# Two-layer graph kernel: the next batch's input rows are turned by VectorE in 32x32 blocks, after a blocked load, instead of by TensorE

## What is computed

```
feats  = einsum(x, W0)                       # 8 heads x 64 units
e      = leaky_relu(self_i + neigh_j, 0.2);  att = softmax(e where adj)
x1     = layernorm(x + relu(att @ feats + b))
agg    = (adj @ x1) / max(deg, eps)
out    = layernorm(x1 + relu([x1, agg] @ W1.T))
```

## Time and profile before

| | us |
|---|---|
| three runs | 3256.30, 3260.62, 3260.65; median 3260.62 |
| the profiled execution's own time | 3259.45 |
| its span, first to last instruction | 3257.7 |
| PE busy, of the span | 3198.1 |
| DVE busy | 2351.7 |
| ACT busy | 2095.9 |
| mean granted TensorE clock | 0.997 |

### The profile page before, as it was taken

One profiled execution on the slowest core, in us unless ns is written; L12 is line 12 of the kernel. 1 busy time (PEld: TensorE's weight loads), 2 busy tenths in 40 slices (PEclk: granted clock), 3 DMA queues, 4 the chain that ended last, 5 costly groups with the idle time before them and its releaser, 6 DMA issues.

```text
span 3257.7 us, 124901 instructions
## 1 busy us (share of the span) xinstructions
PE 3198.1 (98%) x56896; PEld 2698.7 (83%) x56896; DVE 2351.7 (72%) x4272; ACT 2095.9 (64%) x2712; POOL 283.6 (9%) x251
## 2 busy tenths in 40 slices
PE   7999999999999999999999999999999999999998
PEld 6969789697896978979788797987969879697895
DVE  6858678586785857859588585876858768586685
ACT  5748567485674947749477494765837658485583
POOL 0010200102011020100202002020020200202001
PEclk8999999999999999999999999999999999999999
DMA  6143151431524225251242513415144251331512
GB/s 217 58 114 102 51 159 66 109 98 51 154 68 118 87 60 157 62 133 65 78 141 63 140 56 94 129 58 146 51 102 120 58 147 62 102 115 51 140 33 49
DMA packets 368657, 314.52 MB, mean 97 GB/s; under 512 B 285056, under 2 KB 285056, under 8 KB 368128
## 3 DMA queue, kind: packets, MB, share of 16 engines
q1 hardware_dynamic: 368128, 306.52, 33.8%
HBM read 205.26 MB, written 34.08 MB: 73 GB/s over the span
## 4 chain that ended last, share of the span: by engine, by line
PE 89%; DVE 6%; issue 2%; ACT 2%; DMA 1%; SPq 0%; DVEq 0%; POOL 0%; ACTq 0%
PE six L940 77%; PE pair L940 11%; DVE mask L769 2%; PE six L964 1%; DVE rest L674 1%; PE pair L964 1%; DVE x_parts L669 1%; ACT step L512 1%; DMA s_bc<-self_scores 1%; ACT trh L477 0%; DVE x_parts L697 0%; DVE trl L708 0%; DMA self_scores<-sc_row 0%; DVE feat L699 0%; DVE trl L905 0%
## 5 line engine op out<-in xcount | busy, mean ns | idle before, releaser
L940 PE MATMUL six<-rows_bf,mask 128*128 128x65 bf16 x45056 | 1507.8, 193 | 19.3 <-DVE mask L769 12.6
L940 PEld LDWEIGHTS six<-rows_bf,mask 128*128 128x128 fp8e4 x45056 | 1497.6, 97 | 27.5 <-DVE mask L769 16.0
L512 ACT ACTIVATE step<-s_bc,n_step 128x1024 uint16<-128x1024 f32 x1024 | 1090.3, 1136 | 90.7 <-DVE mask L769 71.3
L769 DVE TENSOR_TENSOR mask<-adj_t,step 128x1024 uint16<-128x1024 uint16 x1024 | 655.2, 685 | 47.9 <-ACT step L512 47.4
L940 PE MATMUL six<-adj_t,x_parts 128*128 128x512 fp8e4 x1536 | 385.5, 380 | 11.1 <-DVE trl L905 5.4
L455 POOL TENSOR_TENSOR s_bc<-feat,rden 128x512 f32<-128x512 f32 x112 | 124.1, 1113 | 2721.3 <-DVE s_bc L818 2707.1
L940 PEld LDWEIGHTS six<-adj_t,x_parts 128*128 128x128 f16 x1536 | 145.9, 98 | 201.5 <-DVE trl L905 13.2
L477 ACT ACTIVATE mask<-six,rdeg 128x512 f32<-128x512 f32 x128 | 87.9, 686 | 237.5 <-PE six L940 237.5
L940 PE MATMUL six<-w1h,trh 128*128 128x512 f32 x512 | 211.6, 413 | 0.0
L477 ACT ACTIVATE trh<-six 128x512 fp32r<-128x512 f32 x160 | 87.9, 598 | 184.5 <-PE six L940 162.4
L940 PE MATMUL six<-w1h,trl 128*128 128x512 f32 x512 | 201.0, 392 | 0.0
(11 more groups left out here) (127 smaller groups left out, 4922.8 us busy)
## 6 DMA issues: line engine op xcount, KB each, us to landing
s_bc<-self_scores SPq DMA_DIRECT2D x128, 512.0 KB, 3.8
mask<-in_adj_dram SPq DMA_DIRECT2D x64, 512.0 KB, 4.1
adj_nat<-in_adj_dram SPq DMA_DIRECT2D x64, 512.0 KB, 3.5
xs<-in_x_dram SPq DMA_DIRECT2D x128, 256.0 KB, 3.9
out_dram<-mask SPq DMA_DIRECT2D x128, 256.0 KB, 3.3
adj_nat<-in_x_dram SPq DMA_DIRECT2D x64, 256.0 KB, 5.8
step<-in_x_dram SPq DMA_DIRECT2D x64, 256.0 KB, 4.2
xs<-in_L_gnn_W_dram SPq DMA_DIRECT2D x1, 2048.0 KB, 13.2
```

Of the source, the lines that this page charges most:

```text
L512: act.activation(step[:, g % STEP_SLOTS], s_bc[:, h % 2], ACT.Sigmoid, scale=STEP, bias=n_step[:, jt, h:h + 1]).then_inc(stepped.sem, 1)
L769: dve.tensor_tensor(mask[:, g % MASK_SLOTS], adj_t[:, jt, :], step[:, g % STEP_SLOTS], ALU.logical_shift_left).then_inc(masked.sem, 1)
L940: return pe.matmul(o, l, r, start=start, stop=stop, skip_group_check=True)
```

## The change

Each load of an x tile for turning becomes 4 loads, one for each 128 features, into 32 partitions each: partition 32k + r gets, for i = 0 to 3, row 32i + r of features 128k to 128k + 127, in runs of 512 bytes. DVE's `transpose` in place then turns each 32x32 block of the 128x512 tile. The result has features {128k + 32c + j} on partition 32k + j of chunk c, so layer one's weights are loaded in that order: 16 loads instead of 4. `x_high` and `x_low` read the turned tile in SBUF; PE's `turn_x` is gone. Of DVE's and ACT's order: the block turn stands behind mask 13, 21, 29 and 37, `x_high` behind step g + 5, `x_low` behind mask g + 2, where each had stood at other places before. In the tail DVE's turns stand in `ln1(t)` for t = 1, 2, 5, 6. In the prologue DVE turns tiles 0 to 3 ahead of the weights' split, and 4 to 7 behind the first feature rows.

```diff
-    XT_BANKS = (6, 7, 6, 7, 0, 1, 0, 1)
-    TURN_AT = (10, 13, 18, 21)
+    TURN_AT = (13, 21, 29, 37)
+    SPLIT_BEHIND = 2
+    TAIL_TURN_AT = (1, 2, 5, 6)
+    Q = P // KC
...
+        def turned_rows(t):
+            rows_of = lead_x[:, t] if t < HALF else tail_x[:, t - HALF]
+            return rows_of.rearrange("p (i c r) -> p c i r", i=KC, c=KC)
+        def by_blocks(rows_of):
+            return rows_of.rearrange("p c (i r) -> p c i r", i=KC)
...
+            def load_blocks(rows_of, b, t, landed):
+                for k in range(KC):
+                    sp.dma_start(rows_of[k * Q:(k + 1) * Q].rearrange("p (i f) -> p i f", i=KC),
+                                 x[b, t * P:(t + 1) * P, col(k)].rearrange("(i r) f -> r i f", i=KC)
+                                 ).then_inc(landed.sem, 16)
...
             for c in range(KC):
-                sp.dma_start(w_raw[:, c, :].rearrange("p (h u) -> p h u", h=H),
-                             gat_w[:, col(c), :].rearrange("h p u -> p h u")).then_inc(w_in[0], 16)
+                for k in range(KC):
+                    features_at = k * P + c * Q
+                    sp.dma_start(w_raw[k * Q:(k + 1) * Q, c, :].rearrange("p (h u) -> p h u", h=H),
+                                 gat_w[:, features_at:features_at + Q, :].rearrange("h p u -> p h u")
+                                 ).then_inc(w_in[0], 16)
...
             for s in range(2):
-                sp.wait_ge(xt_ps.sem, xt_ps.at(0, 2 * s + 2))
+                sp.wait_ge(xt_lo.sem, xt_lo.at(0, 2 * s + 2))
                 load_adj(0, s)
...
-                    if h in (3, 4):
-                        s = h - 3
-                        sp.wait_ge(xt_ps.sem, xt_ps.at(b + 1, 2 * s + 2))
+                    if h in (4, 6):
+                        s = h // 2 - 2
+                        sp.wait_ge(xt_lo.sem, xt_lo.at(b + 1, 2 * s + 2))
                         load_adj(b + 1, s)
...
             def x_high(b, t):
-                act.wait_ge(xt_ps.sem, xt_ps.at(b, t + 1))
-                copy(trh[:, :, col(t % HALF)],
-                     bank[XT_BANKS[t]][:].rearrange("p (k n) -> p k n", k=KC)).then_inc(xt_hi.sem, 1)
+                act.wait_ge(x_turned_ok.sem, x_turned_ok.at(b, t + 1))
+                copy(by_blocks(trh[:, :, col(t % HALF)]), turned_rows(t)).then_inc(xt_hi.sem, 1)
...
+            def turn_blocks(b, t):
+                source, landed = (lead_x[:, t], lead_in[t]) if t < HALF else (tail_x[:, t - HALF], tail_in[t - HALF])
+                dve.wait_ge(landed.sem, landed.at(b, 16 * KC))
+                dve.transpose(source, source).then_inc(x_turned_ok.sem, 1)
...
                     mask_word(g)
-                    if more and g - 7 in TURN_AT:
-                        x_low(b + 1, TURN_AT.index(g - 7))
+                    if more and g in TURN_AT:
+                        turn_blocks(b + 1, TURN_AT.index(g))
+                    if more and g - SPLIT_BEHIND in TURN_AT:
+                        x_low(b + 1, TURN_AT.index(g - SPLIT_BEHIND))
```

More of the change, by code:

```diff
@@ L69, in gat_sage_kernel @@
     W1_BANKS = (2, 3)
-    XT_BANKS = (6, 7, 6, 7, 0, 1, 0, 1)
     FT_BANKS = (0, 1, 4, 5, 4, 6, 4, 5)
     MAX_BANK = 3
-    TURN_AT = (10, 13, 18, 21)
+    TURN_AT = (13, 21, 29, 37)
+    SPLIT_BEHIND = 2
+    TAIL_TURN_AT = (1, 2, 5, 6)
+    Q = P // KC
+    assert Q == 32
     FIRST, SECOND = slice(0, HALF), slice(HALF, T)
@@ L216, in gat_sage_kernel @@
         x_in = [Signal(sem(f"x_in{t}"), 16) for t in range(T)]
-        lead_in = [Signal(sem(f"lead_in{t}"), 16) for t in range(HALF)]
-        tail_in = [Signal(sem(f"tail_in{t}"), 16) for t in range(HALF)]
+        lead_in = [Signal(sem(f"lead_in{t}"), 16 * KC) for t in range(HALF)]
+        tail_in = [Signal(sem(f"tail_in{t}"), 16 * KC) for t in range(HALF)]
         a_in = [Signal(sem(f"a_in{s}"), 32) for s in range(4)]
@@ L224, in signal @@
             return Signal(sem(name), per_batch)
-        xt_ps = signal("xt_ps", T)
+        x_turned_ok = signal("x_turned_ok", T)
         xt_hi = signal("xt_hi", T)
@@ L309, in _ @@
         def _(sp):
+            def load_blocks(rows_of, b, t, landed):
[3 more added lines that the diff above has]
+                                 ).then_inc(landed.sem, 16)
             def load_lead(b, t):
-                sp.dma_start(lead_x[:, t, :], x[b, t * P:(t + 1) * P, :]).then_inc(lead_in[t].sem, 16)
+                load_blocks(lead_x[:, t, :], b, t, lead_in[t])
             load_lead(0, 0)
             for c in range(KC):
-                sp.dma_start(w_raw[:, c, :].rearrange("p (h u) -> p h u", h=H),
-                             gat_w[:, col(c), :].rearrange("h p u -> p h u")).then_inc(w_in[0], 16)
+                for k in range(KC):
[3 more added lines that the diff above has]
+                                 ).then_inc(w_in[0], 16)
             for t in range(1, HALF):
@@ L328, in load_tail @@
             def load_tail(b, t):
-                sp.dma_start(tail_x[:, t - HALF, :], x[b, t * P:(t + 1) * P, :]).then_inc(tail_in[t - HALF].sem, 16)
+                load_blocks(tail_x[:, t - HALF, :], b, t, tail_in[t - HALF])
             def load_adj(b, t):
@@ L541, in batch @@
                     make_step(g)
-                    if more and g - 9 in TURN_AT:
-                        if g - 9 == TURN_AT[0]:
+                    turned_at = g - STEP_SLOTS - 1
+                    if more and turned_at in TURN_AT:
+                        if turned_at == TURN_AT[0]:
                             act.wait_ge(ft_ps.sem, ft_ps.at(b, T))
-                        x_high(b + 1, TURN_AT.index(g - 9))
+                        x_high(b + 1, TURN_AT.index(turned_at))
                 def x1_parts_of(t):
@@ L632, in _, with weight_parts @@
         def _(dve):
[L634 to L637, removed]
+            def weight_parts():
+                dve.wait_ge(w_in[0], 16 * KC * KC)
+                dve.tensor_copy(w0h[:], w_raw).then_inc(w_ready, 1)
+                dve.wait_ge(w_ready, 1)
+                dve.tensor_tensor(w0l[:], w_raw, w0h[:].bitcast(F32), ALU.subtract).then_inc(w_ready, 1)
             def attention_weights():
@@ L707, in x_low @@
                 c = t % HALF
-                dve.tensor_tensor(trl[:, :, col(c)], bank[XT_BANKS[t]][:].rearrange("p (k n) -> p k n", k=KC),
-                                  trh[:, :, col(c)].bitcast(F32), ALU.subtract).then_inc(xt_lo.sem, 1)
+                dve.tensor_tensor(by_blocks(trl[:, :, col(c)]), turned_rows(t),
+                                  by_blocks(trh[:, :, col(c)]).bitcast(F32), ALU.subtract).then_inc(xt_lo.sem, 1)
             def feature_rows(b, t):
@@ L882, in ln1 @@
                         x_low(b + 1, T - 1)
+                    if more and t in TAIL_TURN_AT:
+                        turn_blocks(b + 1, HALF + TAIL_TURN_AT.index(t))
                     dve.wait_ge(o2_sb.sem, o2_sb.at(b, t + 1))
@@ L922, in _ @@
             for t in range(HALF):
+                turn_blocks(0, t)
+            weight_parts()
+            for t in range(HALF):
                 x_low(0, t)
@@ L928, in _ @@
                 feature_rows(0, t)
+            for t in range(HALF, T):
+                turn_blocks(0, t)
             for t in range(HALF, T):
@@ L956, in split_product @@
                 return ins
[L958 to L965, removed]
             def features(b, t, chunks=range(KC)):
@@ L1039, in batch @@
                     for jt in range(T):
-                        if more and h * T + jt in TURN_AT:
-                            turn_x(b + 1, TURN_AT.index(h * T + jt))
                         if h < 2 and jt == HALF:
@@ L1129, in batch @@
                         own(t + 1)
[L1130 to L1133, removed]
             pe.wait_ge(consts, N_CONST)
-            for t in range(HALF):
-                turn_x(0, t)
             pe.wait_ge(w_ready, 2)
@@ L1143, in _ @@
             pe.wait_ge(ft_sb.sem, ft_sb.at(0, 2))
-            for t in range(HALF, T):
-                turn_x(0, t)
             pe.wait_ge(w_in[3], 16)
```

## The result

The changed kernel takes 3266.73 us against 3259.88 (medians of 20 runs each), a ratio of 1.0021 with a 95% interval of 1.0014 to 1.0028: 0.2% slower. One of the changed kernel's 20 runs had a granted clock of 0.782 and took 3735.49 us; the ratio leaves it out, and without it the median is 3266.41. The forecast was +11 us; it is +6.9, and +10.5 between the two profiled spans (3268.2 and 3257.7).

What follows compares the result with a forecast made beforehand. The prediction took PE as the bound, with DVE setting its pace between key tiles 13 and 29. Key tiles +26, tail -24 and prologue +8 on 3259.45 gave 3269.5, as a median 3271 us; range 3248 to 3306.

Steps and rivals of the forecast that it cites:

- The bound: Key tiles 13 to 29: DVE sets PE's pace there; removing the turns is worth at most 2.4 us a batch.
- Key tiles: Key tile stage: DVE waits 1.22 us for `x_high`, a turned head takes 12.66 us; +1.75 a batch, +26 us.
- second way of reckoning: Key tiles: 93.9 without turns plus 4 x (12.66 - 11.6) gives 98.1 against 96.3 us, +1.8 a batch.
- The block turn: DVE's transpose of 128x512 f32: taken as 0.605 us from the nearest row, bounds 0.27 and 1.24.
- Rival (B): DVE in turned heads: the block turn takes twice as long, 1.24 us; 38 us more, 3309 us; chance 0.14.
- the estimate 0.65: DVE's block turn by the Trainium skill's figure: 0.65 us, which would make the sum 2.7 us higher.
- Tail: Tail of each batch: four PE turns of 0.44 us go; -1.6 us a batch, x 15 = -24 us.
- Rival (A): Key tiles: DVE's 11.43 us a head fits under PE's 11.6, all PE turns are won; 3206 us; chance 0.14.
- SP's queue: Load queue: 24 more loads a batch, the tail's 16 at 0.44 us each, cost nothing.
- rival (C): Tail: the 16 loads, at 0.79 us or more each, hold up x1; 1.4 us a batch, 3292 us; chance 0.08.
- Prologue: Start, once: 36 more loads ahead of adjacency tiles 0 and 1, first words near 29.7; +8 us, 0 to +13.
- The sum: Whole kernel: 3259.45 + 26 - 24 + 8 = 3269.5 for the profiled execution, 3271 us as median.

Runs made afterwards that it cites:

- split4: The changed kernel with `x_low` two masks later, behind mask g + 4 instead of g + 2: 3214.10 us, ratio 0.9856 to the kernel before.
- split5: The changed kernel with `x_low` behind mask g + 5 instead of g + 2: 3208.95 us, ratio 0.9845 to the kernel before.
- tail_only: The kernel before with only tiles 4 to 7 loaded in blocks and turned by DVE, weights in their old order: 3235.16 us, ratio 0.9920.
- loads_only: The kernel before, PE turns kept, with each x tile for turning in 4 loads and layer one's weights in 16: 3270.64 us, ratio 1.0031.
- extra_pass: The changed kernel with one more 128x512 DVE pass behind each block turn among the key tiles: 3303.56 us, ratio 1.0132 to the kernel before.

## Why the prediction held, point by point

- *The bound.* Right: the stage between the turns is where DVE sets PE's pace. In the kernel before, PE's waits for a mask lie where the working put them, most of them ahead of tile 29 (up to 1.1 us of idle time). The last batch's key tiles, 93.9 us, served as the measure of that stage without turns; with the wait gone the 15 batches come within 0.6 us of it, block turns and all. It is a rough measure: the last batch takes 93.2 to 97.7 us over the twelve profiles, with idle times of PE that end with nothing the profile shows.
- *Key tiles.* Forecast +1.75 us a batch from a turned head of 12.66 us; measured +1.50, heads of 12.61. Batch 4 alone is 98.0, as the second way of reckoning had it (98.1). The rise of the mean is smaller, since the kernel before takes 0.45 us more in its mean batch (96.75) than in batch 4, which the working took for all, and the changed kernel only 0.25 more (98.25).
- *The block turn.* Taken as 0.605 from the nearest form; 0.63 to the next instruction. Rival (B), twice as long, is out. With the wait gone, turning on VectorE wins 45 to 51 us here (`split4`, `split5`), as PE is the bound and VectorE has room. The figure of the Trainium skill (VectorE: DVE Perf Modes, The three transpose paths) let one work out the estimate 0.65; 0.63 lies between it and 0.605. The same page of the Trainium skill (Rules for kernel authors) sends a full 128x128 transpose to TensorE, and its section on the paths has VectorE turn 32x32 blocks only. Here the blocked load supplies the rest of the transpose, so the rule did not tell against the change.
- *Tail.* Forecast -1.6 us a batch; measured -1.59, and -1.65 alone (`tail_only`).
- *Rival (A), DVE keeps up.* Its sum of work, 11.43 us, is confirmed as 11.40; what it lacks in the change is two masks of distance. With them the time is 3214, near its 3206. Its condition (`x_high` ready in time) was right, and the change as it stands doesn't meet it.
- *SP's queue.* A term mis-sized without harm: the tail's 16 loads in batch 4 take 9.86 us, 0.62 each, not 0.44. They end at 975.82, 2.9 us ahead of x1's transposes at 978.70, which start 5.3 us after the last key tile's last matmul as before (968.15 after 962.9):

```profile
965.96 9.86 SPq L327 DMA_DIRECT2D step<-in_x_dram  x16
975.86 0.91 SPq L359 DMA_DIRECT2D mask<-in_adj_dram  x2
978.70 4.26 SPq L371 DMA_TRANSPOSE rest<-x_parts  x2
```

  `loads_only` shows the 24 extra loads a batch at no cost (tails 104.01 against 104.03), so rival (C) is out. Its margin was smaller than the prediction says: by its own bound of 968.15 - 0.8 it begins at 0.75 us a load, not 0.79.
- *Prologue.* Forecast +8, measured +10.5, between the +8 and the upper end of +13. The issue of 53 loads at 0.48 us was right, to 26.2 (26.19 measured). What was too small is the time from there to landing, taken as 3.5 us; the words start 6.1 us after the issue. The prediction also followed the first words, while the start follows the fourth, which wait for a transpose behind layer two's weight. And an equal price for every load is off in its parts: the 12 extra tail loads alone cost 1.2 us, since the loads behind them landed 8.3 us after their issue in the kernel before and 5.3 us in `tail_only`; moving the 16 weight loads off the queue gives back 8.0.
- *The sum.* 26 - 24 + 8 = +10; by the trace 22.5 - 23.9 + 10.5 + 1.6 = +10.7; by the medians +6.9, as the profiled execution of the changed kernel (3269.99 us) is 3.3 above its median and that of the kernel before 0.4 below its own. The sum is nearer than its terms: 3.5 too much among the key tiles against 2.5 too little in the prologue and 1.6 in no term, which is luck in part. The 1.6 behind the last key tile shows in two of the twelve profiles, the changed kernel's and `extra_pass`'s, and it is the granted clock of that one execution. The same work in the last batch, in the changed kernel and in `split4` (from:to, length, busy times; behind POOL's the granted clock), and one matmul of each:

```profile
3199.70:3206.00 6.30, 6.29 (x21) 3.88 (x22) 1.66 (x4) 3.00 (x5) 2.32 (x2) 0.73 0.19 44
3201.68 0.63 PE L981 MATMUL six<-w1l,x1t_h 128*128 128x512 f32 x1
```

```profile
3141.05:3147.35 6.30, 6.28 (x28) 3.75 (x29) 1.67 (x4) 3.02 (x5) 2.32 (x2) 1.00 0.20 44
3142.78 0.39 PE L981 MATMUL six<-w1l,x1t_h 128*128 128x512 f32 x1
```

  A granted clock of 0.73 is a mix of the two levels, 1.2 and 2.4 GHz, and PE starts 21 matmuls there instead of 28; in `extra_pass` it is 0.73 and 21 too. In both kernels PE had waited 1.9 us just before (for `x1t_l`), so why the clock fell in one execution and not in the other is not shown.

## What to carry to other kernels

When work moves from the bound engine to one with room on average, draw up one period of the stage in which it lands, each engine's instructions from start to start, with the waits between them: here the work fitted (11.4 under 11.6 us), and a wait of 1.1 us that two engines made for each other took all of the gain. Such a wait has a remedy that cost nothing here, distance: put the consumer behind as many independent instructions as the producer's chain takes. And where one queue feeds the start of a kernel, count the issues ahead of the load that the start waits for, and find out which load that is: 16 small issues fewer ahead of it brought the start 8.0 us forward, and 5.6 us off the first words alone brought 1.4. A second queue, idle at that time, took the 16 over at no cost that shows.

## What the runs showed of the hardware

- VectorE's transpose in place of 32x32 blocks takes 0.70 us for 128x512 f32, and the next instruction starts 0.63 us after its start, 0.03 more than behind a mask (0.60).
- A DMA of 64 KB costs 0.45 to 0.49 us of SP's queue in the prologue (1.82 us for four, 7.83 for sixteen) and 0.62 in the middle of a batch (9.86 for sixteen); from ACT's queue 0.50 (7.95 for sixteen), and the two queues issue at the same time.
- ACT copies 128x512 f32 from SBUF in 615 to 621 ns (means of 64 copies each, changed kernel), against 586 to 598 ns from PSUM (means of 96 and 160, kernel before).
- A 2 MB load in the prologue lands 9.2 to 13.2 us after its issue, and the words that wait for the first DMA transpose behind it start 1.0 to 1.3 us after that, in all six versions of the table.
- With the granted clock at 1.2 GHz a 128x512 f32 matmul is listed with 0.63 us, at 2.4 GHz with 0.39.
